# A cross-interaction network on one core: quad 1 without GpSimd additions, with its own places for quad 2's and quad 3's layer 0

## The reference

```
Xi = einsum('hjk,bjd,bkd->bhd', W.reshape(128, 39, Fi), X0, Xi) + b[None, :, None]
res.append(Xi.sum(axis=2))
```

## Time and profile before

| | |
|---|---|
| median of 3 runs | 698.75 us (696.44 to 703.89) |
| profiled execution | 701.35 us, span from first to last instruction 699.5 us |
| granted TensorE clock, mean | 0.983 |
| PE busy | 666.5 us (95%) |
| ACT busy | 566.5 us (81%) |
| DVE busy | 507.4 us (73%) |
| POOL busy | 454.9 us (65%) |
| DMA | 46.02 MB, 66 GB/s mean |

### The profile page before, as it was taken

One profiled execution on the slowest core, in us unless ns is written; L12 is line 12 of the kernel. 1 busy time (PEld: TensorE's weight loads), 2 busy tenths in 40 slices (PEclk: granted clock), 3 DMA queues, 4 the chain that ended last, 5 costly groups with the idle time before them and its releaser, 6 DMA issues.

```text
span 699.5 us, 10372 instructions
## 1 busy us (share of the span) xinstructions
PE 666.5 (95%) x2686; PEld 492.0 (70%) x2686; DVE 507.4 (73%) x977; ACT 566.5 (81%) x1997; POOL 454.9 (65%) x445
## 2 busy tenths in 40 slices
PE   4297889999999999999999999999999999999998
PEld 4275657777777777777777777777777777776683
DVE  5266667787777777877777788777777787888690
ACT  3266578889888888988888888898988888999672
POOL 7728547877787777788787877787887736432000
PEclk9789999999999999999999999999999999999999
DMA  6023241323433323233231313131213122004300
GB/s 205 14 64 98 37 96 34 96 37 96 97 95 81 108 25 110 35 90 71 73 88 6 96 7 95 8 94 8 95 6 97 5 84 85 2 1 148 145 1 0
DMA packets 107532, 46.02 MB, mean 66 GB/s; under 512 B 80897, under 2 KB 92941, under 8 KB 107474
## 3 DMA queue, kind: packets, MB, share of 16 engines
q1 hardware_dynamic: 101427, 42.82, 23.1%
q0 software_dynamic: 5120, 1.29, 2.2%
q10 hardware_dynamic: 927, 1.26, 0.6%
HBM read 13.81 MB, written 5.24 MB: 27 GB/s over the span
## 4 chain that ended last, share of the span: by engine, by line
PE 90%; ACT 3%; another core or an unknown queue 2%; DVE 2%; DMA 1%; issue 1%; POOL 0%; SPq 0%; ACTq 0%; DVEq 0%
PE ps_y L913 21%; PE ps_y L915 20%; PE ps_y L914 20%; PE ps_x L841 13%; PE ps_g L930 5%; PE ps_tr L810 2%; ACT prod L556 2%; PE ps_y L974 1%; PE ps_y L975 1%; PE ps_y L976 1%; PE ps_y L988 1%; PE ps_y L924 1%; PE ps_tr L818 1%; DMA g_all<-in_L_rec_W 1%
## 5 line engine op out<-in xcount | busy, mean ns | idle before, releaser
L556 ACT ACTIVATE prod<-ps_y,xt 128x128 f32<-128x128 f32 x1792 | 492.8, 440 | 81.7 <-PE ps_y L915 69.1
L913 PE MATMUL ps_y<-w_hi,x_hi 128*128 128x512 f32 (+1 forms) x640 | 313.5, 490 | 7.8 <-ACT prod L556 5.6
L915 PE MATMUL ps_y<-w_hi,x_lo 128*128 128x512 f32 (+1 forms) x640 | 249.9, 390 | 0.0
L914 PE MATMUL ps_y<-w_lo,x_hi 128*128 128x512 f32 (+1 forms) x640 | 249.8, 390 | 0.0
L417 POOL TENSOR_TENSOR prod<-prod 128x512 f32<-128x512 f32 x120 | 154.8, 1290 | 113.9 <-ACT prod L556 106.4
L737 DVE SCALAR_TENSOR_TENSOR prod<-ps_y,xt,prod 128x128 f32<-128x128 f32 x576 | 164.4, 344 | 52.5 <-PE ps_y L915 44.6
L388 POOL DMA_INDIRECT rows<-in_table,index x160 | 156.3, 977 | 39.2 <-issue 32.6
L913 PEld LDWEIGHTS ps_y<-w_hi,x_hi 128*128 128x128 f32 x640 | 121.2, 189 | 65.6 <-issue 21.1
L744 DVE TENSOR_REDUCE prod<-prod 128x128 f32<-128x1536 f32 (+1 forms) x64 | 116.3, 1817 | 63.5 <-ACT prod L556 63.5
L914 PEld LDWEIGHTS ps_y<-w_lo,x_hi 128*128 128x128 f32 x640 | 121.3, 190 | 47.6 <-issue 24.2
L412 POOL TENSOR_TENSOR room<-room 117x512 f32<-117x512 f32 (+1 forms) x105 | 134.9, 1289 | 19.7 <-DMA room<-room 19.6
(11 more groups left out here) (118 smaller groups left out, 327.0 us busy)
## 6 DMA issues: line engine op xcount, KB each, us to landing
room<-room SPq DMA_DIRECT2D x75, 234.0 KB
room<-room SPq DMA_DIRECT2D x45, 78.0 KB
emb_room<-rows SPq DMA_DIRECT2D x168, 5.0 KB
rows<-in_table,index POOLq DMA_INDIRECT x160
w_hi_dram<-g_all SPq DMA_DIRECT2D x5, 512.0 KB
w_lo_dram<-g_all SPq DMA_DIRECT2D x5, 512.0 KB
room<-room SPq DMA_DIRECT2D x15, 156.0 KB
g_all<-in_L_rec_W SPq DMA_DIRECT2D x9, 256.0 KB, 5.8
```

The lines of the kernel that those rows point to most:

```text
L556: ins = nc.scalar.activation(prod[:, SLOT[k] + m // 2, :, m % 2], ps_y[:, g % YBANKS, m * H:(m + 1) * H], ACT.Copy, scale=xt[:, q % 2, ti, ...
L913: nc.tensor.matmul(y, hi, w1_hi[:, cols], start=True, stop=False)
L914: nc.tensor.matmul(y, hi, w1_lo[:, cols], start=False, stop=False)
L915: nc.tensor.matmul(y, lo, w1_hi[:, cols], start=False, stop=True).then_inc(y_made, 1)
```

## The change

A constant `FREE_QUADS = 2` takes the place of "quad 0" in several conditions, so quad 1 (tiles 4 to 7) now also has no additions on POOL and DVE's long early reduction. Quad 2's rows are turned after (4, 7) and copied after (4, 7), where they were turned after (2, 9) and copied after (3, 0). Quad 3's rows are turned after (7, 2) and copied after (7, 6), where it was (6, 4) and (6, 6). Quad 1 now uses the second table for the chunks of quad 2, so the first stands after (5, 9) and not after (4, 2); quad 3's chunks keep their places in quad 2. POOL's part without additions is longer: after the gathers of quad 3 it issues six gathers of quad 4, then all products of quad 2, the last four gathers of quad 4, the repeat for quad 3 and products 0 and 1 of quad 3. The loads of layer 2's weights come one quad later, and their turns, which alternated between ti = 3 and the next ti = 0, alternate between ti = 0 and ti = 3, the first in tile 8 instead of tile 7.

```diff
+FREE_QUADS = 2
-THIRD_TURNED_AFTER, THIRD_KEPT_AFTER = (2, 9), (3, 0)
+THIRD_TURNED_AFTER, THIRD_KEPT_AFTER = (3, 2), (3, 6)
...
-SECOND_REGROUPED_AFTER, SECOND_TURNED_AFTER, SECOND_KEPT_AFTER = 3, 7, 7
+SECOND_REGROUPED_AFTER = 3
+NEXT_TURNED_AFTER, NEXT_KEPT_AFTER = (0, 7), (0, 7)
...
-W2_TURNED_IN = {QT * (n // 2 + 1 + n % 2) + (0 if n % 2 else 3): n for n in range(W2_GROUPS)}
+W2_TURNED_IN = {QT * (n // 2 + 2) + (3 if n % 2 else 0): n for n in range(W2_GROUPS)}
...
-                if q <= W2_PARTS:
-                    if q == 1:
+                if 0 <= q - 2 < W2_PARTS:
+                    if q == 2:
                         sp.wait_ge(prep_tr, len(TURNS))
-                    load_w2(q - 1)
+                    load_w2(q - 2)
...
             make_index(3)
-            for g in range(4):
+            for g in range(GATHERS):
+                if g == 4:
+                    repeat_rows(2)
                 gather(3, g)
-            repeat_rows(2)
-            for g in range(4, GATHERS):
-                gather(3, g)
+            make_index(4)
+            for g in range(6):
+                gather(4, g)
+            for c in range(CHUNKS):
+                multiply(2, c)
+            for g in range(6, GATHERS):
+                gather(4, g)
+            repeat_rows(3)
             for c in MULTIPLIED_AHEAD[3, 1]:
-                multiply(2, c)
+                multiply(3, c)
...
-            for T in range(QT, TILES):
+            for T in range(FREE_QUADS * QT, TILES):
                 for part in range(2):
                     add_groups(T, part)
...
-                    if (T, g) == (0, SECOND_KEPT_AFTER):
-                        keep_x0(1)
-                    if q + 2 < QUADS and (ti, g) == (KEPT_AFTER if q > 0 else THIRD_KEPT_AFTER):
+                    if q < FREE_QUADS and (ti, g) == NEXT_KEPT_AFTER:
+                        keep_x0(q + 1)
+                    if FREE_QUADS - 1 <= q < QUADS - 2 and (ti, g) == (KEPT_AFTER if q >= FREE_QUADS else THIRD_KEPT_AFTER):
                         keep_x0(q + 2)
...
-                wait(dve, pool_step, len(ADDED) * (T + 1 - QT))
+                wait(dve, pool_step, len(ADDED) * (T + 1 - FREE_QUADS * QT))
...
-                pe.wait_ge(x0_made, T // QT + 3 if n % 2 == 0 else T // QT + 2)
+                pe.wait_ge(x0_made, T // QT + (2 if T % QT == 0 else 3))
...
-                    if (T, g) == (0, SECOND_TURNED_AFTER):
-                        turn_rows(1)
-                    if q + 2 < QUADS and (ti, g) == (TURNED_AFTER if q > 0 else THIRD_TURNED_AFTER):
+                    if q < FREE_QUADS and (ti, g) == NEXT_TURNED_AFTER:
+                        turn_rows(q + 1)
+                    if FREE_QUADS - 1 <= q < QUADS - 2 and (ti, g) == (TURNED_AFTER if q >= FREE_QUADS else THIRD_TURNED_AFTER):
                         turn_rows(q + 2)
-                    order = SUMMED_AFTER if q > 0 else SECOND_SUMMED_AFTER
+                    order = SUMMED_AFTER if q >= FREE_QUADS else SECOND_SUMMED_AFTER
```

More of the change, by code:

```diff
@@ L424, in _ @@
             pool.wait_ge(ids_ld, 32)
[L425 to L428, removed]
+            make_index(0)
+            for g in range(GATHERS):
+                gather(0, g)
+            make_index(1)
+            for g in range(GATHERS):
+                gather(1, g)
             pool.wait_ge(gathered[1], 16 * GATHERS)
@@ L741, in reduce_early @@
                 dve.wait_ge(act_step, ACT_STEPS * T + 5)
-                wait(dve, pool_step, len(ADDED) * (T + 1 - QT))
+                wait(dve, pool_step, len(ADDED) * (T + 1 - FREE_QUADS * QT))
                 wait(dve, reduced, REDUCTIONS * T)
-                nc.vector.tensor_reduce(prod[:, BIASED, :, 0], prod[:, EARLY if T >= QT else EARLY_FIRST].rearrange("p n h l -> p h n l"), AX_XY,
+                nc.vector.tensor_reduce(prod[:, BIASED, :, 0], prod[:, EARLY if T >= FREE_QUADS * QT else EARLY_FIRST].rearrange("p n h l -> p h n l"), AX_XY,
                                         ALU.add).then_inc(reduced, 1)
```

## The result

The changed kernel takes **715.83 us** (median of 4 runs, 715.19 to 718.38) against 699.12 for the kernel before on the same chip; the ratio is **1.0237**, with a 95% interval of 1.0205 to 1.0269. The forecast was 715. The profiled execution took 716.04 us, its span is 714.2 (699.5 before), and the mean granted clock fell from 0.983 to 0.967.

What follows compares the result with a forecast made beforehand. TensorE was taken as the bound, busy 535.84 of 536.00 us from 104 us on. Terms 5.5 + 0.8 - 0.75 + 2.7 + 6.8 + 1.6 = 16.65 on 698.75 gave 715.4; range 704 to 721 for 8 in 10.

Steps and rivals of the forecast that it cites:

- Part 1: Tile 3: sixteen gathers in one run hold TensorE's finished-signals longer, so group 0 of tile 4 starts later, +5.5 us.
- (4,0) at 95 to 98: Sign to look for: group 0 of tile 4 starts at 95 to 98 us, instead of 90.89.
- Part 2: Quad 2's turn moves from (2,9) to (4,7), where nothing hides it on TensorE: +0.8 us.
- Parts 3 and 4: Tile 4's wait on GpSimd goes, that on VectorE grows, -0.75 us; quad 2's chunk 1 waits for its windows, +2.7.
- part 7: Fewer additions, VectorE's longer early reduction in tiles 4 to 7, and layer 2's later weight loads and turns: free or nearly so.
- Part 5: Tile 8: quad 3's later turn makes TensorE wait 2.8 us for chunk 0 and 4.0 for chunk 1, +6.8.
- part 6: Clock: the longer waits in tiles 3 and 8 may each bring a fall to half; one priced, +1.6 us.
- Rival A: Tile 3: gathers do not hold the signals longer, the delay belongs to something else; 708.5 us, chance 0.22.
- Rival B: Chunk 1 in tile 8: windows land in time, within about 5 us, so not slower; 698.2 us, chance 0.05.
- Rival C: Tiles 4 to 7: VectorE becomes the bound, 4.2 us on top; 719.6 us, chance 0.07.

Runs made afterwards that it cites:

- the pauses: The changed kernel, with quad 4's six gathers made to wait, two at a time, for ScalarE's steps in tile 4: 709.46 us, ratio 1.0135.
- the long run alone: The kernel before, with only quad 4's six gathers moved directly behind quad 3's ten: 705.83 us against 698.91, ratio 1.0098.
- all of it: The changed kernel with gathers of quads 1 to 4 broken up, quad 3's products and chunks later, quad 2's turn earlier in tile 4: 692.37 us, ratio 0.9885.
- the late chunks: The changed kernel, with quad 3's chunks on TensorE from (9,9) on instead of (8,2), GpSimd's queue unchanged: 718.22 us, ratio 1.0284.
- the products one place earlier: The kernel of all of it, with quad 3's products 1 and 3 moved ahead of additions in tiles 9 and 10: 692.31 us, ratio 0.9871.

## Why the prediction was right, and which terms were not

The direction, the two places and the time held. The forecast of 715.4 was 0.4 us below the median, and that it came so close is luck. Between the medians the time grew by 16.7 us, where the sum has 16.65; but between the two profiled executions, from which the terms below are read, it grew by 14.7, and the terms that were off partly cancelled. One sum among the chances is wrong: the forecast, C and two thirds of A make 0.88 and not 0.84.

**Part 1 (+5.5 forecast) was too small by some 1.5, and the clock's fall in tile 3 came on top.** Tile 3 grew by 9.46 us, though the run became only 7.8 us longer (90.70 against 82.91), where 8 were expected. The prediction let some three groups through. Only one group of tile 3, (3,0), was read during the run; the reads stand at 79.18, 85.57 and 90.52. So ScalarE had three groups left at 93.37, and not two at 92.7. Behind them came, as forecast, the copy of quad 1's x1 and VectorE's split of it, on which (4,0) waits:

```profile
97.19 0.75 DVE L681 SCALAR_TENSOR_TENSOR x_lo<-ps_x,columns,x_hi 128x512 fp32r<-128x512 f32 x1 [1.67 <-ACT x_hi L506]
```

It ended at 97.94, 7.05 us after the 90.89 at which (4,0) began before, and inside the part's range. But (4,0) began at 100.29: TensorE had run out of PSUM banks early, its clock was at 1.2 GHz from 86.3 to 99.8, and it was still at work on tile 3. At full clock the 5.7 us of work from 94.58 on would have taken about half (an estimate) and been done before the split. So of the 9.4 us by which (4,0) came later, 7.05 are part 1's and 2.35 the clock's. That the run is the cause is shown by two opposite edits: put in alone it costs 6.9 us, broken up it gives back 6.4. "(4,0) at 95 to 98" was missed, at 100.29.

**Part 2 (+0.8) can't be read by itself.** The turn takes 0.70 us of TensorE in tile 4. Tile 3 starts at the same time without it (78.91 and 78.98), but that doesn't show that it was free before: tile 2 takes 1.0 us less without it, and tile 1, where the two kernels do the same, 1.4 more. What it adds in tile 4 is inside the -0.86 of tiles 4 to 7.

**Parts 3 and 4 (-0.75 and +2.7) were too dear by some 3.6 us with part 2**: 2.75 forecast, -0.86 measured for all three. The longer wait at (4,3), 1.85, did not come, because TensorE itself came late out of tile 3 and VectorE had caught up; once the pauses are in, it is there (1.74). So that term was right about VectorE and wrong about who would be late. Chunk 1's wait was 1.69 instead of 2.7; of the 1.0, 0.6 is the landing (10.8 us instead of 11.4). With the two old waits gone (-2.60), the turn (0.70) and this wait make -0.2. Another 0.36 is a turn of layer 2's weights, which stood in tile 7 (127.03 to 127.39 in the trace of before) and now stands behind tile 7; part 7 counted that move as nothing. The last 0.3 I can't place.

**Part 5 (+6.8) and part 6 (+1.6) were counted apart and overlapped.** Tile 8 grew by 6.81. The wait for chunk 0 was 3.35 (2.8 forecast), that for chunk 1 only 0.32 (4.0 forecast). Between them TensorE ran at 1.2 GHz, 5.52 us of work of which half, 2.8, is lost to the clock: 3.35 + 0.32 + 2.8 = 6.5. The windows landed when they landed, and a slow TensorE that would have waited anyway loses nothing. A fall of the clock ahead of a wait for a fixed time is not an extra term. The fall that did cost is the one in tile 3, 2.35 where 1.6 was priced. Outside tiles 3 to 8 the two traces differ by -0.7: tiles 9 to 62 take 1.0 more, and from the start of the last tile on it is 1.6 less (62.86 us before, 61.23 after), because the clock fell near 652 us in the trace of before and did not in that of after.

**Rival A (708.5, chance 0.22)** is refuted by the long run alone. The Trainium skill, SBUF — State Buffer (Who interferes with whom), by whose rule it held, speaks of ports to the memory and does not cover this case: taken for the whole of TensorE and ScalarE, as the rival took it, the trace disagrees, for ScalarE read finished work of TensorE 10.7 us late while GpSimd issued gathers. In the same run ScalarE's own signals were not late (see below). Which path carries TensorE's signals and what of a gather holds it, no run here shows; that stays open. **Rival B (698.2)** is refuted by the landings, 10.8 and 10.9 us, where it needed about 5. The fit of the Trainium skill, DMA: Bandwidth & Descriptors (Anatomy of one DMA), is for one DMA on GpSimd's path; used as an estimate for these nine copies together, which go through SP's queue, it would give 5.6, and the trace disagrees here as it did before. **Rival C (719.6)** did not come: no wait of TensorE in tiles 4 to 7 of the kernel after was ended by VectorE; where the other waits are gone, it holds TensorE up by 1.74 at (4,3) with the pauses alone, and by 1.17 at (5,3) and 1.15 at (8,3) with all of it.

## What to carry to other kernels

Break long runs of indirect DMAs on GpSimd with waits on another engine's progress: here that alone, with one product of GpSimd moved to break a run, took 1.1% off a kernel whose busiest engine was never GpSimd. Look in the trace whether a pause holds at all: one that waits for a step that is already past lets the run go on, as with quad 4's six gathers. When a turn or a load moves later, move everything that stands behind its transfers in the same in-order queue with it; moving only the consumer (the late chunks) moved the wait to tile 9, and made it longer, through additions queued behind a waiting product. And don't add a lower clock to a wait whose end is fixed by a transfer: the slower work fills the wait.

## What the runs showed of the hardware

- A matmul group that ended at 79.78 us was read at 90.52, with the reader idle for 3.80 us ahead of it. During a run of gathers the reads come singly, 6.4 and 5.0 us apart; 2.7 us after the last gather of the changed kernel three groups were read without a gap, 3.3 us after it in the long run put in alone, and 1.7 us after the shorter one.
- In the same run of gathers ScalarE's own signals were not late. It ended its read of (2,9) at 86.72 (85.57 + 1.15), and VectorE's second reduction, which waits for that read, began at 86.75, as TensorE's next group did at 86.77:

```profile
86.75 1.75 DVE L764 TENSOR_REDUCE x<-prod 128x128 f32<-128x1536 f32 x1 [3.90 <-ACT prod L568]
```

- From 160 us on, where at most four gathers stand in a row between additions and products, TensorE is idle for 0.21 of 495 us. With the pauses' result this says that it is the unbroken run, not the number of gathers, that holds the signals. How short a run must be isn't settled: behind six in a row (5,0) was still read 2.8 us late in the trace of the products one place earlier.
- Nine copies within SBUF for one quad's windows, 1560 KB, landed 10.8 and 10.9 us after the first was issued, in two other tiles than before and in nearly the same time (11.4 and 11.6 before).
